# Half of the probability tiles turned by VectorE and a trip through memory, and a new order for the plain steps

## The reference

```python
def _L1_xattn_ref(hidden_states, encoder_hidden_states, Wq, Wk, Wv, Wo, gq, gk):   # 16 heads of 128
    q = rmsnorm((hidden_states @ Wq).reshape(B, Sq, H, D), gq)
    k = rmsnorm((encoder_hidden_states @ Wk).reshape(B, Skv, H, D), gk)
    v = (encoder_hidden_states @ Wv).reshape(B, Skv, H, D)
    attn = jax.nn.softmax(jnp.einsum('bqhd,bkhd->bhqk', q, k) * scale, axis=-1)
    out = jnp.einsum('bhqk,bkhd->bqhd', attn, v)
    return out.reshape(B, Sq, H * D) @ Wo

x = x + jnp.tanh(g_xattn[1]) * _L1_xattn_ref(_layernorm(x), ctx_1024, ...)
x = x + jnp.tanh(g_ffn[1]) * _L1_ffn_ref(_layernorm(x), topk_idx, topk_weight, ...)   # 16 experts, 4 per token
```

## Time and profile before

| | |
|---|---|
| runs | 1462.61, 1465.05, 1465.51 us (median 1465.05) |
| profiled execution: span of the trace | 1461.5 us; no other time is given for it |
| PE busy, DVE, ACT, POOL | 1437.8, 1107.0, 977.5, 864.5 us |
| chain that ended last | PE 82%, DVE 7%, ACT 4%, POOL 4% |
| granted clock of PE | 0.998 mean |
| bytes moved | 142.74 MB, mean 98 GB/s |

### The profile page before, as it was taken

The page is one execution under the profiler, slowest core; times in us unless marked ns, Lnnn a source line. Parts: engine busy times, 40 slices in busy tenths (PEclk is TensorE's granted clock), DMA queues, the critical chain, the costliest instruction groups (busy, mean ns, idle before and its releaser), DMA issues.

```text
span 1461.5 us, 23763 instructions
## 1 busy us (share of the span) xinstructions
PE 1437.8 (98%) x8086; PEld 1223.0 (84%) x8086; DVE 1107.0 (76%) x2100; ACT 977.5 (67%) x2224; POOL 864.5 (59%) x701
## 2 busy tenths in 40 slices
PE   8999999999999999999999999999999999999998
PEld 6778788888888888888888888888888888888887
DVE  7888777777777777777777777777777776787777
ACT  7864477777776667667676767667676765666664
POOL 4785555555554566666575757575666655664341
PEclk9999999999999999999999999999999999999999
DMA  8420011111111333434333433433434331321002
GB/s 325 159 66 16 22 44 45 57 44 44 44 44 44 139 124 126 149 108 147 124 129 127 139 123 127 139 117 132 136 115 144 125 126 36 107 82 37 8 1 87
DMA packets 55495, 142.74 MB, mean 98 GB/s; under 512 B 5392, under 2 KB 5392, under 8 KB 55376
## 3 DMA queue, kind: packets, MB, share of 16 engines
q1 hardware_dynamic: 51616, 128.90, 26.1%
q0 software_dynamic: 3760, 12.32, 3.0%
HBM read 126.79 MB, written 14.42 MB: 97 GB/s over the span
## 4 chain that ended last, share of the span: by engine, by line
PE 82%; DVE 7%; ACT 4%; POOL 4%; issue 2%; DMA 0%; ACTq 0%; SPq 0%; DVEq 0%; POOLq 0%
PE w_bank L505 10%; PE w_bank L507 10%; PE w_bank L506 10%; PE j_bank L505 9%; PE j_bank L507 9%; PE j_bank L506 9%; PE t_bank L573 7%; PE s_bank L505 4%; PE s_bank L507 4%; PE s_bank L506 4%; PE t_bank L538 2%; POOL q_scale L1855 2%; POOL wo_lo L1815 2%; ACT prob L927 1%; PE t_bank L657 1%
## 5 line engine op out<-in xcount | busy, mean ns | idle before, releaser
L927 ACT ACTIVATE prob<-s_bank,neg_bias,q_scale 128x512 f32<-128x512 f32 x255 | 198.0, 777 | 186.5 <-DVE neg_bias L1422 186.4
L1262 DVE TENSOR_TENSOR probT_lo<-t_bank,probT_hi 128x512 fp32r<-128x512 f32 x260 | 176.4, 689 | 168.4 <-ACT probT_hi L892 168.4
L1476 DVE SCALAR_TENSOR_TENSOR x_sb<-w_bank,inv_sum,x_sb 128x512 f32<-128x512 f32 x254 | 188.4, 744 | 0.0
L1401 DVE TENSOR_REDUCE neg_max<-s_bank 128x1 f32<-128x512 f32 x255 | 168.6, 682 | 0.9 <-PE s_bank L507 0.9
L1815 POOL TENSOR_TENSOR xnT_lo<-xnT_raw,xnT_hi 128x512 fp32r<-128x512 f32 (+2 forms) x47 | 126.5, 2693 | 61.5 <-ACT xnT_hi L892 61.5
L573 PE MATMUL t_bank<-ident,prob 128*128 128x128 f32 x1008 | 151.4, 273 | 1.3 <-ACT prob L927 1.1
L892 ACT CAST probT_hi<-t_bank 128x512 fp32r<-128x512 f32 x260 | 150.1, 590 | 1.8 <-PE t_bank L515 1.8
L1855 POOL TENSOR_TENSOR q_scale<-q_ss,minus_half 128x4 f32<-128x4 f32 x64 | 65.9, 1030 | 143.6 <-DVE q_ss L1414 143.6
L505 PE MATMUL j_bank<-wkv_lo,cT_hi 128*128 128x256 f32 x512 | 145.1, 283 | 0.7 <-DVE oT_lo L1262 0.4
L507 PE MATMUL j_bank<-wkv_hi,cT_lo 128*128 128x256 f32 x512 | 144.6, 282 | 0.0
L506 PE MATMUL j_bank<-wkv_hi,cT_hi 128*128 128x256 f32 x512 | 144.4, 282 | 0.0
(11 more groups left out here) (308 smaller groups left out, 4454.2 us busy)
## 6 DMA issues: line engine op xcount, KB each, us to landing
stage<-w SPq DMA_DIRECT2D x96, 256.0 KB, 3.4
xnT_raw<-w_gu SPq DMA_DIRECT2D x31, 704.0 KB, 4.8
cT_raw<-w_gu SPq DMA_DIRECT2D x31, 704.0 KB, 4.7
xnT_raw<-w_dn SPq DMA_DIRECT2D x16, 768.0 KB, 4.4
cT_raw<-w_dn SPq DMA_DIRECT2D x15, 768.0 KB, 4.7
planes<-bits SPq DMA_DIRECT2D x16, 512.0 KB, 4.8
y<-stage SPq DMA_DIRECT2D x31, 256.0 KB, 4.0
x_sb<-x SPq DMA_DIRECT2D x5, 1024.0 KB, 10.9
```

Source lines behind the costliest of these rows:

```text
L927: nc.scalar.activation(prob[:, i, :], score_bank(t, i)[:], ACT.Exp, bias=neg_bias[:, u % 2, i:i + 1], scale=q_scale[:, u % 2, i:i + 1], ac ...
L1262: return nc.vector.tensor_tensor(dst, src, hi, ALU.subtract)
L1401: nc.vector.tensor_reduce(neg_max[:, u % 2, i:i + 1], score_bank(t, i)[:], AX_X, ALU.max, negate=True).then_inc(own_max, 1)
L1476: nc.vector.scalar_tensor_tensor(out=here, in0=w_bank[0][:] if packed else out_bank(t, i)[:], scalar=inv_sum[:, w % 2, i:i + 1], in1=here, ...
```

## The change

Of the four probability tiles of an item, tiles 0 and 1 are no longer turned on PE (`moved(u)`: the items 2 to 61, steps 3 to 62, 60 of them). In their place:

1. ACT writes the exponentials of these two tiles with the keys in a permuted order (pieces of 32).
2. DVE turns 32x32 squares of both tiles in place, one instruction of 128x1024 (`turn_quads`).
3. SP stores both tiles in memory (`store_pair`, 512 KB) and, when that has landed, loads them back in four transfers of 128 KB, each to 32 partitions in runs of 512 bytes (`load_pair`).
4. ACT makes the high part of both in one 128x1024 copy (`moved_hi`), POOL the low part in one 128x1024 subtraction (`moved_lo`). Before, ACT and DVE had done it tile by tile from PSUM.

`probT` gets another layout for this, and the value product reads it in runs of 32 with a stride. In plain steps the value product goes behind keys and values on PE and into another bank; scores 2 and 3 follow it; the lists of ACT and DVE for plain steps are written in a new order to match. ACT and POOL split the key and value weights of a new head one step earlier in plain steps. In packed steps DVE takes the squares out one place earlier, `squares_out` ahead of `rows_to_lo`. SP puts the store of the pair ahead of the down weights of a packed step and the loads behind them.

The core of the diff:

```diff
+def moved(u):
+    return 3 <= u + 1 < NI - 1
+def turned_tiles(u):
+    return (2, 3) if moved(u) else range(NT)
...
+            def store_pair(u):
+                sp.wait_ge(p_quads, MOVES[u] + 1)
+                wait(sp, p_moved, 16 * NT * MOVES[u])
+                sp.dma_start(turn_dram.rearrange("i p m -> p i m"), prob_pair).then_inc(p_stored, 16)
+            def load_pair(u):
+                sp.wait_ge(p_stored, 16 * (MOVES[u] + 1))
+                for c in range(NT):
+                    sp.dma_start(prob[c * QUAD:(c + 1) * QUAD, 0:2, :].rearrange("a i (r m) -> a (i r) m", r=NT),
+                                 turn_dram.rearrange("i (r a) (c m) -> c a (i r) m", r=NT, c=NT)[c]).then_inc(p_moved, 16)
...
+                if in_block(t):
+                    store_pair(t - 1)
+                    down_weights(b, e)
+                    load_pair(t - 1)
...
+                if not in_block(t):
+                    store_pair(t - 1)
+                    load_pair(t - 1)
...
                 def values():
-                    need(pe, p_lo, 4, w, 4)
+                    wait(pe, p_lo, TILES[w + 1])
+                    wait(pe, pair_lo, MOVES[w + 1])
...
+                if not packed:
+                    query_squares()
+                    project_down()
+                    key_value(0)
+                    late_turn()
+                    key_value(1)
+                    values()
+                    if t == 2:
+                        table()
+                    scores(2)
+                    scores(3)
+                    project_out(0)
+                    probs(0)
+                    project_out(1)
+                    probs(1)
+                    query((0, 1))
+                    probs(2)
+                    query((2, 3))
+                    key_turn()
+                    project_out(2)
+                    probs(3)
+                    project_out(3)
+                    return
...
+                def moved_hi(v):
+                    act.wait_ge(p_moved, 16 * NT * (MOVES[v] + 1))
+                    need(act, pv_mm, 1, v - 1, 1)
+                    copy_hi(probT_pair(0), prob_pair).then_inc(pair_hi, 1)
...
                 late_norm()
+                if not in_block(t - 1):
+                    moved_hi(w)
...
+                def turn_quads():
+                    need(dve, p_exp, 4, u, 2)
+                    flat_pair = prob_pair.rearrange("p i s -> p (i s)")
+                    nc.vector.transpose(flat_pair, flat_pair).then_inc(p_quads, 1)
...
+                def moved_lo(v):
+                    pool.wait_ge(pair_hi, MOVES[v] + 1)
+                    lower(probT_pair(1), prob_pair, f32(probT_pair(0))).then_inc(pair_lo, 1)
...
                 if up:
                     take_rows(b + 1)
+                moved_lo(w)
                 query_scale()
```

More of the change, by code:

```diff
@@ L474, in _ @@
                     gate_up_weights(0, 0, e)
[L475 to L481, removed]
                 if 0 <= b < NB - 1:
@@ L534, in turn_keys @@
                     need(pe, q_ss_out, 1, 0, 1)
+                elif moved(t - 1):
+                    need(pe, q_ss_out, 1, t - 1, 1)
                 elif t:
-                    need(pe, p_lo, 4, t - 1, 2)
+                    wait(pe, p_lo, TILES[t - 1] + 2)
                 for j in range(NT):
@@ L569, in probs @@
                         need(pe, p_lo, 4, u, (0, None, 0, 1)[i])
+                    elif moved(u):
+                        wait(pe, p_lo, TILES[u] + i - 2)
+                        if i == 2 and not packed:
+                            need(pe, o_lo, 1, w, 1)
                     elif t != LAST_SCORES:
-                        need(pe, p_lo, 4, u, (0, None, 1, 3)[i])
+                        wait(pe, p_lo, TILES[u] + (0, None, 1, 3)[i])
                     for j in range(4):
@@ L626, in key_value @@
                         need(pe, q_squared, 2, u, 2)
-                    elif value:
+                    elif packed:
                         need(pe, o_lo, 1, w, 1)
@@ L661, in table @@
                     pe.wait_ge(place_ready, 1 + NT)
-                    need(pe, p_lo, 4, 0, 4)
+                    wait(pe, p_lo, TILES[1])
                     for c in range(PAIRS):
@@ L782, in step @@
                 scores(1)
-                if not (up and down):
+                if not packed:
+                    query_squares()
[19 more added lines that the diff above has]
+                    project_out(3)
+                    return
+                if not down:
                     query_squares()
@@ new lines, in step @@
+                if t == T0 - 1:
+                    dve.wait_ge(x0_out, 16)
+                    dve.wait_ge(rstd_ready, NMOMENTS // NT + 1)
+                    normalised(0)
+                    normalised(1)
+                turn_quads()
+                if t == 2:
+                    tokens()
+                values_lo()
+                take(0)
+                if t == T0 - 2:
+                    statistics(0, 1, NMOMENTS + 1)
+                maximum(2)
+                shift(2)
+                maximum(3)
@@ L2066 @@
     x0 = nc.dram_tensor("x0", (S, D), F32, kind="Internal").ap()
-    flamingo_kernel(nc, *args, x0, rows, y, out)
+    turn = nc.dram_tensor("turn", (2, P, S), F32, kind="Internal").ap()
+    flamingo_kernel(nc, *args, x0, rows, y, turn, out)
     result = run_bass_kernel_spmd(nc, [arrays], core_ids=[0])
```

289 lines of the change are left out of this document (154 added, 135 removed).

## The result

The changed kernel takes 1592.57 us (median of 4 runs, 1587.17 to 1594.25) against 1465.28 for the kernel before, measured beside it: ratio 1.087, 95% interval 1.085 to 1.089. It is slower, as forecast, but by 127 us instead of 75, and 2.6 us above the end of the range.

A forecast was written before the change was run, and what follows sets the result against it. PE bounds the kernel before; after the change, POOL's pair was to bound packed steps. Span 1461.5 + 85 (packed) - 10 (plain) = 1536.5, plus 3.55 for runs above the span: 1540 us, range 1490 to 1590.

The forecast's parts named there:

- the mechanism: Packed steps: the pair's way through POOL is the bound, a loop of 24.8 us against 22.6 of PE's work; chance 0.70.
- the ordinary step: Packed step without a new head, 21 of the 31: 25.8 us forecast, against 23.48 before.
- The rival of a trip that is the bound: Store and loads through memory land late on the shared queue; at R = 11, 1608 us; chance 0.12.
- The 19-fold loss: Skill's warning that a plain copy whose access pattern does the transposing is 19 times slower than the crossbar's; given no time.
- PE waits 2.2 us ahead of each value product: Packed steps: PE waits for the pair's low part from POOL, loop 24.8 us against 22.6 of PE's work.
- The sum: Whole kernel: 1461.5 + 85 for packed steps - 10 for plain steps = 1536.5 against the profiled span.
- Weights of a new head one step earlier in plain steps: Plain steps: work moved from ahead of the keys to idle time, costed at nothing.
- the held-up engine: Packed steps: POOL's `moved_lo` waits while DVE does its 1408-wide subtraction; 0 to 1.4 us, taken as 1.0.
- About covers: Packed steps: down weights asked for some 1.4 us later, which ACT's place for them behind both last exponentials about covers.
- 7.7 + R: Plain steps: loop through softmax and memory, R the store-and-load round trip of 9.3 us; 17.0 us, -10 us over 29 steps.
- about 15.7: Plain steps: PE's own work in us after the change, 16.1 with a late tile.

## Why the prediction was right and wrong

**Right: the mechanism and the ordinary step.** I measured each piece of the loop from one value product to the next in the changed kernel, means of 8 to 10 loops of each kind (us):

| piece | forecast | ordinary | into a new-head step | out of one |
|---|---|---|---|---|
| value product to query copy | 16.74 | 17.1 | 18.0 | 19.2 |
| query copy to the pair's copy | 0.97 | 1.3 | 1.2 | 1.0 |
| to the first square | 0.93 | 0.95 | 0.95 | 0.95 |
| to `squares_lo` | 1.2 | 1.17 | 1.17 | 1.17 |
| to the pair's subtraction | 2.5, new head 3.8 | 2.54 | 4.99 | 2.54 |
| to the value product | 2.46 | 2.46 | 2.46 | 2.47 |

From the pair's copy on, the pieces on ACT and POOL are right to 0.1 us, but for the fetch in a new-head step, and the experiment with the pair ahead of the fetch showed them to be the bound: 66 us came back. The first piece is 0.9 us longer into a new-head step than in an ordinary one; PE's rows show 0.37 of it as a wait for an exponential and 0.19 as one for POOL's scaled keys, and the rest was not followed. The rival of a trip that is the bound (0.12) is refuted by the run without the trip. ACT waited for the loads 4 times in 60, 6.5 us in all. The 19-fold loss that the Trainium skill gives for a copy whose access pattern does the transposing (VectorE: DVE Perf Modes, The three transpose paths) did not appear here, where DVE turns the squares and the copy keeps runs of 512 bytes.

**Wrong: "PE waits 2.2 us ahead of each value product" was costed at its own length.** The waits were 1.4 us in an ordinary step and 3.9 in one with a new head. A wait of 3.9 us in a new-head step was followed by products at half the clock, 2.2 us more in that step (last column: 19.2 for 16.9 in the run with PE kept busy). Ten steps make 22 us, and filling the wait gave 24.5. This is about half of the miss; without it the time lies inside the range. Step 20 has the same in it: PE waited 5.02 us for the squares and then 3.70 for the pair, and the granted clock was 0.50 from 491.0 to 504.7. The sum had no term for the clock at all. In steps 1 to 62 of the kernel before PE never waited longer than 0.82 us, but its layer 0 shows the effect: a wait of 2.10 us, and soon behind it products 0.43 us apart.

```profile
51.16 0.47 PE L505 MATMUL w_bank<-probT_lo,xnT_hi 128*128 128x512 f32 x1 [2.10 <-DVE x_sb L1761]
...
52.94 0.63 PE L505 MATMUL w_bank<-probT_lo,xnT_hi 128*128 128x512 f32 x1
53.37 0.63 PE L506 MATMUL w_bank<-probT_hi,xnT_hi 128*128 128x512 f32 x1
```

**Wrong: "Weights of a new head one step earlier in plain steps" at nothing.** This edit and others at the edges, which the sum did not name, are some 9 of the 19 us outside the packed steps, as the run with the edges mended shows. Without the 19 us, too, the time lies inside the range. In step 1 POOL makes the next key weights ahead of the squares that PE waits for (3.77 us); in step 2 the table is later (1.16); in step 19 DVE's new list normalises two of the fetched rows' tiles later, their store goes out later, POOL waits for it ahead of the squares, and PE for them (5.02, above). I looked at the regular steps only. Mending these places and the pair's place in step 20 gave 10 us. Steps 51 to 62 lost theirs in steps 53 and 55 to 58 and were not mended. Step 53 is the trip's, by the run without it; steps 55 to 58 took the same 17.9 to 18.0 us there, and their cause stays open.

**Wrong place: the held-up engine.** I added 1.0 us to each step for POOL's pair behind DVE's first weights. In ordinary steps POOL was there first and nothing was added to the loop (2.46); DVE was held instead:

```profile
824.40 4.18 DVE L1369 TENSOR_TENSOR xnT_lo<-xnT_raw,xnT_hi 128x1408 fp32r<-128x1408 f32 x1
```

That is 1.6 us of work and a wait for POOL's fetch (to 824.68) and pair (to 827.09). In new-head steps the fetch was held, 2.26 for 1.05, which makes the 4.99 of the table. The ordinary loop came out at 25.5 us (24.8 + 1.0 forecast) all the same, by 0.4 and 0.3 us elsewhere in it: the 25.8 is right by errors that cancel, which is luck. The Trainium skill (SBUF — State Buffer, Who interferes with whom) has this exclusion for whole instructions; both rows agree.

**Too low: the down weights.** "About covers" was wrong: they came 1.3 us late in each step. It mattered little, 9 and 11 us by two runs, because the loop through POOL is longer.

**Plain steps: 17.0, by the wrong reason.** Steps 4 to 15 took 17.02 us, but my loop of "7.7 + R" through memory did not set them: without the trip they took the same 17.02. PE itself was busy for 16.8 of them, with one wait of 0.16 for the squares, so it is PE's own work that sets them, as it did the 17.6 before (17.5 busy). My "about 15.7" for that work has no rows behind it: 17.49 less the 0.88 of the earlier trace rows is 16.6. The 17.0 is luck.

## What to carry to other kernels

A wait that a change puts on the engine that sets the pace costs its own length and, if it is long enough (3.9 us here, never 1.4), the clock behind it: look for one that repeats, and if it can't be removed, price it by filling it with work that nobody reads. An operation moved off the busiest engine pays only if its last piece is on an engine that is free at that moment: here the same subtraction cost 93 us on POOL and allowed a gain on DVE, where it takes half as long. And an edit that looks free in the regular steps must be followed through the first and last steps one by one.

## What was not expected of the hardware

- The granted clock fell to 1.2 GHz in a kernel whose PE is busy 91% of the time, behind single waits of 3.9 us. Behind waits of 1.4 us it never did; behind waits of 1.9 to 2.0 it did in some steps and not in others.
- Taking away one wait (down weights, 32 us on ACT) brought another there (first weights, 20 us), lengthened a third on PE, and the clock fell in steps where it had not: 9 us in the time.
- A 128x1024 subtraction took 2.40 us on POOL and 1.23 on DVE; a 128x1408 one on DVE took 4.18 us instead of 1.61 when two POOL instructions ran first.
- 81600 more packets for 63 MB left most landings on the queue as they were: 3.2 us for weights of 256 KB, with 3.4 before, and 4.8 for the first weights of 704 KB, as before. The down weights of 768 KB landed later, 5.4 and 5.5 us with 4.4 and 4.7, and the stores of `y` sooner, 2.0 with 4.0.
